# Shared expert moved in the order of two engines, a power moved among scatters, another row order, other output transfers

## The reference

```python
x = x + tanh(g_xattn[0]) * xattn0(layernorm(x), ctx, ctx)     # softmax over features
x = x + tanh(g_ffn[0])   * ffn0(layernorm(x), ...)            # ternary weights, top 102 of 1024, layernorm
x = x + tanh(g_xattn[1]) * xattn1(ctx, ctx, layernorm(x), ssm_kernel, D, 8)
x = x + tanh(g_ffn[1])   * moe(layernorm(x), ...)

# xattn1, per head h of 16 (8 of the 128 positions each), over the 256 features as the sequence l
kv  = einsum('bhil,bhjl->bijhl', k, v)
out = causal_conv(kv, ssm_kernel[h]) + kv * D[h]
out = einsum('bijhl,bhil->bjhl', out, q)

# moe over 2048 tokens: 64 experts, 6 per token, hidden 176, and a shared expert of hidden 352
scores = softmax(x @ gate_w.T); w6, id6 = top_k(scores, 6); w6 = w6 / sum(w6)
routed = sum over the 6 of w6 * (silu(g) * u) @ w_down[e]
shared = (silu(x @ wsg.T) * (x @ wsu.T)) @ ws_down.T
out    = routed + shared
```

## Time and profile before

| | us |
|---|---|
| median of 3 runs (lowest, highest) | 900.29 (899.45, 901.83) |
| profiled execution, its own time | 894.96 |
| span of the profiled execution | 893.2 |
| PE, DVE, ACT, POOL busy in the span | 650.9, 566.1, 252.7, 469.2 |

### The profile page before, as it was taken

One profiled execution on the slowest core, in us unless ns is written; L12 is line 12 of the kernel. 1 busy time (PEld: TensorE's weight loads), 2 busy tenths in 40 slices (PEclk: granted clock), 3 DMA queues, 4 the chain that ended last, 5 costly groups with the idle time before them and its releaser, 6 DMA issues.

```text
span 893.2 us, 12357 instructions
## 1 busy us (share of the span) xinstructions
PE 650.9 (73%) x2938; PEld 508.3 (57%) x2938; DVE 566.1 (63%) x1772; ACT 252.7 (28%) x559; POOL 469.2 (53%) x505
## 2 busy tenths in 40 slices
PE   2378994000199866688888778999999999999930
PEld 1244551000187754466666557888888888888820
DVE  3788875999868877988888463444444444444431
ACT  1113435677023320122322222222222222222200
POOL 4358884662022220266666653666666666666642
PEclk9589998555599998899999699999999999999975
DMA  7335557883000207355442524999999999999877
GB/s 271 122 108 177 200 181 274 328 337 135 1 12 24 87 30 245 105 166 182 160 157 82 181 82 140 220 234 219 231 238 221 229 233 223 231 230 227 174 181 188
DMA packets 85089, 157.77 MB, mean 177 GB/s; under 512 B 10944, under 2 KB 55424, under 8 KB 85056
## 3 DMA queue, kind: packets, MB, share of 16 engines
q1 hardware_dynamic: 54400, 103.23, 35.9%
q0 software_dynamic: 29792, 53.25, 25.1%
q10 hardware_dynamic: 864, 0.93, 0.3%
HBM read 88.66 MB, written 68.70 MB: 176 GB/s over the span
## 4 chain that ended last, share of the span: by engine, by line
PE 54%; DVE 23%; issue 8%; DMA 6%; POOL 4%; DVEq 1%; SPq 1%; ACT 1%; POOLq 0%; ACTq 0%
PE psum L958 11%; PE psum L750 7%; PE psum L971 6%; PE psum L973 6%; PE psum L962 6%; PE psum L946 3%; POOL xs_rows L649 3%; PE psum L790 3%; PE psum L877 2%; DVE qT L1340 2%; DVE hh L1387 2%; PE psum L888 2%; DMA Z<-xs_rows 2%; PE psum L732 1%; PE psum L722 1%
## 5 line engine op out<-in xcount | busy, mean ns | idle before, releaser
L683 POOL DMA_INDIRECT acc<-hh,toki x128 | 199.0, 1555 | 113.1 <-DVE hh L1726 53.7
L649 POOL DMA_INDIRECT xs_rows<-Z,slot x96 | 100.3, 1045 | 68.3 <-DVE slot L1584 42.4
L958 PE MATMUL psum<-qT,Z 128*128 128x256 f32 x512 | 121.2, 380 | 0.2 <-ACT qT L1145 0.2
L958 PEld LDWEIGHTS psum<-qT,Z 128*128 128x128 f32 x512 | 92.4, 190 | 10.4 <-issue 0.5
L1726 DVE TENSOR_SCALAR hh<-psum,wtok 128x256 f32<-128x256 f32 x128 | 56.0, 479 | 64.5 <-PE psum L973 51.1
L571 POOL TENSOR_TENSOR rstd<-mv,neghalf 128x1 f32<-128x1 f32 (+1 forms) x48 | 30.7, 640 | 121.3 <-DVE mv L1211 121.3
L1714 DVE TENSOR_TENSOR hh<-H,psum 128x256 f32<-128x256 f32 x64 | 26.9, 421 | 81.9 <-ACT H L1151 81.8
L971 PE MATMUL psum<-Z,hh 128*128 128x256 f32 x256 | 76.2, 379 | 1.2 <-DVE hh L1716 1.2
L973 PE MATMUL psum<-wt,hh 128*128 128x256 f32 x256 | 76.2, 379 | 0.0
L1145 ACT ACTIVATE qT<-psum 128x512 f32<-128x512 f32 x64 | 38.1, 597 | 122.5 <-PE psum L946 122.4
L750 PE MATMUL psum<-wt,hTs 128*128 128x512 f32 x128 | 61.2, 622 | 12.8 <-ACT hTs L1042 7.7
(11 more groups left out here) (295 smaller groups left out, 1368.7 us busy)
## 6 DMA issues: line engine op xcount, KB each, us to landing
Z<-in_wexp SPq DMA_DIRECT2D x66, 496.0 KB, 4.3
xs_rows<-fill POOLq DMA_DIRECT2D x64, 272.0 KB, 2.8
Z<-xs_rows SPq DMA_DIRECT2D x64, 272.0 KB, 3.6
Z<-kv_rows SPq DMA_DIRECT2D x16, 688.0 KB, 4.4
kv_rows<-Z SPq DMA_DIRECT2D x12, 688.0 KB, 3.9
acc<-fill POOLq DMA_DIRECT2D x4, 1024.0 KB, 8.6
ctxH_s<-in_ctxH SPq DMA_DIRECT2D x16, 224.0 KB, 3.9
wt<-in_wd SPq DMA_DIRECT2D x66, 48.0 KB, 4.4
```

What stands on the lines that cost most here:

```text
L649: pool.indirect_dma_start(out=xs_rows[:, :], out_offset=bass.IndirectOffsetOnAxis(ap=slot[:, t, k:k + 1], axis=0), in_=H[:, t, :], in_offs ...
L683: pool.indirect_dma_start(out=acc[s % 2][:, :], out_offset=bass.IndirectOffsetOnAxis(ap=toki[:, g, j:j + 1], axis=0), in_=y_sb[:, s, j, :] ...
L958: m = pe.matmul(pA[par][:, g * CAP:(g + 1) * CAP], wgu_sb[:, s, k, g * P:(g + 1) * P], xT[:, par, k, :], start=(k == 0), stop=(k == 1))
```

## The change

Six edits:

1. PE's list: `shared_down` moves behind `ranks` of the same period and now belongs to pair `w`. Groups 0 and 1 of `shared_up` stand at the end of a period for pair `u`, group 2 in the middle of the next. Before, group 0 came in the middle of a period, groups 1 and 2 at its end, and `shared_down` one period after that. The waits that guard the banks follow.
2. DVE's list: the three `shared_hidden` and `shared_out` of pair `w` all stand in one period, `shared_out` behind `place`; `diag(b + 2)` comes ahead of `one(b)`.
3. ACT's list: the three silus stand together ahead of the copy of the turned tile.
4. POOL's list: `pow_pair(u + 1)` stands behind five scatters of pair `u` instead of six.
5. Rows of a tile by sequence and then position (`b j`): `one` writes 256 columns in one run, and `x_rows` is written in the new order.
6. Output by tiles: 16 transfers of 128 KB, each from all 128 partitions, instead of 32.

```diff
@@ SP
-                sp.dma_start(x_rows.rearrange("(p b) d -> p b d", b=NT)[:, b, :], X[:, b, :]).then_inc(x2_out, 16)
+                sp.dma_start(x_rows.rearrange("(h b j) d -> b h j d", b=NT, j=HD)[b], X[:, b, :]).then_inc(x2_out, 16)
...
-                for j in range(HD):
-                    sp.dma_start(out.rearrange("b (h j) d -> j b h d", j=HD)[j][:, 4 * c:4 * c + 4, :],
-                                 X[j * NT:(j + 1) * NT, 4 * c:4 * c + 4, :]).then_inc(out_done, 16)
-            sp.wait_ge(out_done, 16 * 4 * HD)
+                for t in range(4 * c, 4 * c + 4):
+                    sp.dma_start(out.rearrange("b (h j) d -> h b j d", j=HD)[t], X[:, t, :]).then_inc(out_done, 16)
+            sp.wait_ge(out_done, 16 * NT)
@@ POOL
-                scatter(2 * u)
+                for k in range(K - 1):
+                    scatter(2 * u, k)
                 if u + 1 < NPAIR:
                     pow_pair(u + 1)
-                scatter(2 * u + 1)
+                scatter(2 * u, K - 1)
+                for k in range(K):
+                    scatter(2 * u + 1, k)
@@ PE, x3_turn, r_turns, shared_down
-                if n >= 3:
-                    pe.wait_ge(base_ready, n - 2)
+                if n >= 2:
+                    pe.wait_ge(base_ready, n - 1)
...
-                if u >= 2:
-                    pe.wait_ge(shid_ready, 3 * u - 4)
+                if u >= 1:
+                    pe.wait_ge(shid_ready, 3 * u - 1)
...
-                pe.wait_ge(x3_done, min(2 * w + 6, NT))
+                pe.wait_ge(x3_done, min(2 * w + 4, NT))
@@ PE, the period
-                if w >= 1:
-                    shared_down(w - 1)
                 if w >= 0:
-                    shared_up(w, 0)
+                    shared_up(w, 2)
...
                 if w >= 0:
-                    shared_up(w, 1)
-                    shared_up(w, 2)
+                    shared_down(w)
+                if 0 <= u < NPAIR - 1:
+                    shared_up(u, 0)
+                    shared_up(u, 1)
@@ DVE, one
-                r = prods[:, 0:512].rearrange("p (s l b j) -> p s l b j", s=2, l=2, j=HD)
-                dve.tensor_tensor(OT[:, h % 8].rearrange("p l (j b) -> p l b j", j=HD), r[:, 0], r[:, 1], ALU.add).then_inc(o3_ready, 1)
+                dve.tensor_tensor(OT[:, h % 8].rearrange("p l t -> p (l t)"), prods[:, 0:256], prods[:, 256:512], ALU.add).then_inc(o3_ready, 1)
```

49 lines of the change are left out of this document (20 added, 29 removed).

## The result

| | before | changed |
|---|---|---|
| median of 6 runs, us (lowest, highest) | 901.06 (897.66, 902.84) | 888.10 (886.53, 892.21) |
| profiled execution, us | 894.96 | 886.88 |
| span, us | 893.2 | 885.2 |

A forecast was written before the change was run, and what follows sets the result against it. DVE was taken to bound the heads stage and SP's issue queue the output, PE's experts staying unchanged. Gains of 14.5 up to the experts and 7.4 at the output, 21.9 us, took the median from 900.3 to 878.4; range 873 to 886.

The forecast's parts named there:

- The power, `one` and the shared expert in the periods: Heads stage: earlier power 8.7 us, shorter `one` 1.0, two more `shared_hidden` -0.7, logits waits gone 1.3; 10.3 earlier.
- rival C: Heads periods: `diag` and `one` shut the power out, 0.6 us later in six periods; 3.6 lost, time 882; chance 0.05.
- The end of the stage: Heads stage's end: the last two `slots_ready` 18.7 us apart instead of 21.7, 3.0 gained.
- Behind the last slots: Between last slots and experts: padding waits for scatters, not `shared_out`; PE's 1.23 us idle before first `down` goes; 1.2 gained.
- The output: Output: 16 issues replace 32 at 0.465 us each, SP's issue stays the bound, same landing; 7.4 us gained.
- Rival B: Output: bound by packets, not issue, reported by about 890.1; gain 2.7 us instead of 7.4, time 883.1; chance 0.10.
- A: Tail stays at lower clock: end of stage gains 0.2 us, not 3.0, logits waits stay; time 882.5; chance 0.15.
- D: Tail of the heads stage: full clock there, 3.2 us more gained, time 875.2; chance 0.12.
- E: Heads periods: PE at lower clock between mask and `x3_turn`, `x3_add` 4.6 us late each; slower, time 912; chance 0.04.

The follow-up runs named there:

- e3_power: The kernel before with one edit, POOL's power behind five scatters instead of six: ratio 0.9934 to the kernel before.
- e12_power_back: The changed kernel with POOL's power back behind six scatters, all else as changed: 888.77 us, ratio 0.9832 to the kernel before.
- e2_output: The kernel before with the output alone changed to 16 transfers of one tile each, rows in the old order: ratio 0.9968 to the kernel before.
- e4_shared: The changed kernel without its power edit, row order and output, so only the shared expert moves: ratio 0.99 to the kernel before.

## Why the prediction was right in part and wrong in size

- **The power, `one` and the shared expert in the periods** (8.7, 1.0, -0.7, 1.3; sum 10.3 at the last but one slots): against the first slots they came 9.95 earlier. `normalise` 0.90 behind the moments, period 19.4, `one` 0.42, no logits waits in the periods: all as stated. The split is not. The 8.7 stands under the power, but it is what the power and DVE's new order close together: the power alone wins 4.2 (e3_power), and put back it costs 4.1 (e12_power_back), since DVE's longer list ahead of the moments hides the rest of POOL's lateness by itself.
- **The Trainium skill's page "SBUF — State Buffer", section "Who interferes with whom"** (rival C, the power shut out by `diag` and `one`): the trace does not show it. With `diag` and `one` beside it the power took 0.77 us, where it had 0.72 with DVE idle, and `normalise` starts 0.90 behind the moments.
- **The end of the stage** (18.7 between the last two slots): 18.07, and `x3_turn` ended 9.8 behind the mask, as stated. In part the size of the gain is luck: the 21.7 that it was set against is 19.0 in e2_output, with the same instructions at a higher granted clock. The gain, forecast at 3.0, is 3.6 against the first profile of before and 0.9 against that of e2_output.
- **Behind the last slots** (1.2 gained): this is the step that failed in its mechanism. It took the 28.3 us of the one profile as the kernel's own. "The padding transfers no longer wait for `shared_out` but for the scatters" did not come true, as DVE's counts came 22.3 behind the slots; nor did the first down's idle 1.23 go. In its place stand PE's updates, late while POOL issues scatters back to back. Of the 10.3 us lost between the first two profiles, 7.8 is what before pays too in its second one. So the gain was summed from a profile without the lateness and carried over one to one to runs that, as it seems, have it.
- **The output** (7.4): this term was mis-sized, by 3.0. 16 issues do replace 32, and issue is the bound, but at 0.606 and not 0.43 each: 4.4. The term had the old cost of an issue for a transfer of another form, and named the 0.32 of the old `x_rows` write as the better case. Rival B's landing did not come in the changed kernel (2.4), but in the old row order (e2_output) the transfers did run behind their issues. The rule of the 4 of 16 ports, section "Door 1: The DMA port swizzle" of the same page, changed neither.
- **Rivals.** A and D were about the clock of the tail; it fell and rose there (0.76 from 504 to 526), but the lateness decided. E did not come. A milder form did, in some executions: PE loses the upper level for part of each period, which costs 1.1 us in each from the fourth on, at `shared_out` and not at `x3_add`. No rival has a wait that no engine's work accounts for.

**What the terms leave open.** The second pair of profiles gives 15.2 us (unrounded): 13.8 in the heads stage, -0.2 behind it, 4.4 at the output, and -1.4 and -1.5 in the stages ahead of the first slots and in the experts, which the change leaves all but as they are. In the profiles of all these kernels the experts' stretch is 324.7 to 329.3 us long, so the last two can be what single executions differ by. Against the 21.9 of the sum the output is then the largest miss (3.0), and the tail's is 1.4. How much of the 12 to 13 us of the medians each term holds no run separates.

**Also open** is why the periods show no late update. Their longest unbroken rows are of 4 to 6 scatters, and in the tail three are enough. The length of the row does matter: where the last row is 18 long (the changed kernel and its versions with POOL's list unchanged) the last pair's first silu is 4.2 to 8.6 us late; where it is 12 long (e4_shared, e12_power_back) this silu is on time and later ones are not. In all of them the last of the late updates arrives 3.1 to 4.2 us behind the start of the last scatter.

What singled out the first profile of before is open too. In that one the trace has all 1,536 updates of the scatters' semaphore, in the others 507 to 807 of them. Missing records alone do not go with lateness, since the runs with nothing late have 713 to 807. Whether the recording has a part in the lateness wasn't tried. The Trainium skill, page "NOTIFIC — the notification-queue block", section "7.1 Overflow: three behaviours, one of which stalls the engine", says that the pipeline of such records holds its producers up rather than lose one inside the block, and that an engine can be throttled by it, while a full ring can drop new records. That either happens here no run shows.

## What to carry to other kernels

Profile the kernel before twice, and distrust a profile that lies below all timed runs: here it hid 8 us. Look at the granted clock of a stretch too before its length is taken as given.

Where an engine waits for PE work that has long ended ("remote"), look at what POOL issues at that time, and break up long rows of indirect transfers; a small instruction ahead of each made all updates punctual and cost as much in late scatters as it won. With one ahead of every third the time was 877.5 us instead of 879.8, though the intervals of the two ratios overlap. What is clear of noise is the rest: with the output on two queues, earlier padding and the groups first the ratio went from 0.984 to 0.975.

Take the cost of an issue from a transfer of the same form on both sides, alone or in a burst as yours will stand, and not from the transfer that it replaces. Share a closing burst of issues between two queues.

## What the runs showed of the hardware that was not expected

- Updates of PE's semaphores come up to 11.4 us late while POOL issues scatters of 128 rows 1.27 us apart, and on time at 1.83 or 2.7 apart. DVE's updates arrived at once in the same stretch: PE's L932 starts at 520.96 in the changed kernel, 0.05 behind the end of DVE's `bvals` that it waits for.
- An issue on SP's queue of 128 rows of 1 KB from 128 partitions takes 0.32 us with one regular step in HBM, 0.52 with two nested steps, and 0.60 with two nested steps in a burst; one of 64 rows from 16 partitions takes 0.36 as the first of a burst and 0.426 within it.
- The same heads stage runs at granted clock 1.00 or 0.91 in different executions, with periods of 19.4 or 20.5.
